# Gated cross-attention and a ternary feed-forward on one core: another order of the feed-forward tiles' steps, wider copies, and three products moved

## The chip, the cores and the metric

The kernel runs on one core of one Trainium2 chip. The metric is the device time of one execution in microseconds (us). The core has TensorE (PE; its weight loads are listed as PEld), VectorE (DVE), ScalarE (ACT), GpSimd (POOL) and SyncE (SP, which only issues DMAs here). Each engine takes its own instructions strictly in order; engines wait for one another on semaphores.

## The reference, cut to what matters

```python
# x [32, 224, 512], ctx [32, 750, 384], 16 heads; weights Wq, Wkv, w1 [2048, 512], w2 [512, 2048]
x = x + tanh(g_xattn) * attention(layernorm(x), ctx, mask)      # attention stage
x = x + tanh(g_ffn) * ffn(layernorm(x))                         # feed-forward stage

def bitlinear(x, w, b):
    x = x * rsqrt(mean(x * x) + 1e-5)                           # per row
    s = 127 / clip(max(abs(x)), 1e-5)                           # per row
    xq = clip(round(x * s), -128, 127) / s
    m = clip(mean(abs(w)), 1e-5)
    wq = clip(round(w / m), -1, 1) * m                          # three levels
    return xq @ wq.T + b
ffn = lambda x: bitlinear(gelu(bitlinear(x, w1, b1)), w2, b2)
```

There are 32 x 224 = 7168 rows, so 56 tiles of 128 rows in the feed-forward stage.

## The kernel before, in words

The **attention stage** (the first 1480 us or so) goes batch by batch and writes its rows, not yet gated, to a DRAM tensor `attn_d`. `divided` (L624) ends a batch: VectorE takes reciprocals of the denominators (`rden`, [57, 16]) and multiplies the rows out of PSUM. The last batch's rows, the row of the mean of v that SP spreads over a batch, and then a barrier stand before the next stage.

The **feed-forward stage** (L1116 on) is a software pipeline over the 56 tiles. `run_steps` (L1163) calls each engine's `step(s, j, u)`: some steps written out, a hardware loop of four steps per turn, some steps written out. In step s the work of several tiles is in flight. With k for a tile:

- SP loads x (`xb`) and attention rows (`ab`) of a tile into one of four slots and stores results from two slots of `yo`.
- GpSimd, tile s+2: gates `ab` (L1227), adds it to `xb` to give `x1` (L1229), computes the factor FAC by a power (L1234, L1237), centres the row, `xc` (L1242). Between, it adds the result of tile s-2 (`result`, L1215). For tile s: HR, a power of the mean square (L1246), and `x1b` = x1 + gated b2 (L1250).
- VectorE, tile s: four hidden copies `hid` = PSUM x XDEQ + b1, 512 columns each (L1302); the copy of the turned `xq` of s+1 (L1306) and half that of `hq` of s-1 (L1309); bn_stats and bn_aggr of s+2 (L1313, L1315), -mean (L1317); the maximum of |hid| over 2048 columns (L1321), HMS = mean square + eps (L1324), the maximum of |xc| (L1329); then for both tiles, interleaved, the small [128, 1] chains: CLIP, INV, DEQ, S (L1334 to L1355); and `xq` of s+2, rounded (L1360).
- ScalarE, tile s: four GELUs of 512 columns in place (L1264); the other half of the copy of turned `hq` of s-1 (L1267); the square of `hid` with its sum (L1272); `yo` of s-1 out of PSUM x HDEQ (L1278); `hq` = hid x HS, rounded (L1281).
- TensorE: 16 first matmuls of tile s in four groups of 512 columns (L1379); four transposes of `xq` of s+1 (L1387); 16 transposes of `hq` of s-1 (L1396), and right behind them its second matmul, 16 times 512 columns (L1406).

HDEQ is the clipped maximum / 127 x w_mean x gate; XDEQ the clipped maximum / 127 x w_mean. PSUM's eight banks: four hold the hidden tile, two the turned hq, one y, one the turned xq.

## Time and profile before

| what | us |
|---|---|
| median of 3 runs (lowest, highest) | 2026.45 (2025.77, 2028.01) |
| the profiled execution | 2027.01 |
| its span, first to last instruction | 2025.2 |
| busy in the span: PE / DVE / ACT / POOL | 1890.2 / 1285.2 / 1059.2 / 550.2 |
| granted TensorE clock, mean | 0.987 |

Views used below: the windows (busy time of each engine in a stretch), the timeline (one line per run of instructions of one line of code, with the idle time before it and what ended that in brackets), and the groups by form (one line of code and one shape: count, busy time, mean duration). An instruction can start before the one ahead of it on its engine has ended; so starts tell how long an engine is occupied, durations when a result is there.

### The profile page before, as it was taken

How to read it: one execution, taken by the hardware profiler on the slowest of the kernel's cores; microseconds unless marked ns; L12 is line 12 of the kernel's file. 1: busy time of each engine (PE TensorE's matmuls, PEld its weight loads, DVE VectorE, ACT ScalarE, POOL GpSimd, SP SyncE). 2: the span in 40 equal slices, each digit the busy share in tenths (PEclk: the TensorE clock that was granted, in tenths of full speed). 3: DMA queues.
4: the chain of work that ended last, by engine and by line, in shares of the span. 5: the costliest groups of instructions: out<-in, count | busy, mean ns of one | idle time of the engine just before them, and what ended most of it. 6: DMA issues, size and time to landing. Idle time of an engine off the chain costs nothing. (4 is left out here: it accounts for less than half of the span.)

```text
span 2025.2 us, 39793 instructions
## 1 busy us (share of the span) xinstructions
PE 1890.2 (93%) x13922; PEld 1469.5 (73%) x13923; DVE 1285.2 (63%) x2586; ACT 1059.2 (52%) x1807; POOL 550.2 (27%) x589
## 2 busy tenths in 40 slices
PE   4999999999999999999999999999849898898987
PEld 4888888888888887888888888888724444444444
DVE  3555455455545545555556545555559999999996
ACT  3444444444444443444444444444338888888887
POOL 2101011010101111010102101010037777777774
PEclk9999999999999999999999999999969999999999
DMA  3012111111211111112211111111022222222221
GB/s 123 19 50 80 49 47 42 47 42 49 76 53 47 42 47 43 48 45 60 73 42 47 42 47 42 47 57 47 21 88 79 93 78 93 78 93 83 88 87 49
DMA packets 56104, 120.61 MB, mean 60 GB/s; under 512 B 5597, under 2 KB 5597, under 8 KB 55934
## 3 DMA queue, kind: packets, MB, share of 16 engines
q1 hardware_dynamic: 56062, 120.07, 18.5%
q8 instruction: 24, 0.39, 0.1%
q14 instruction: 18, 0.15, 0.0%
HBM read 101.64 MB, written 29.43 MB: 65 GB/s over the span
## 5 line engine op out<-in xcount | busy, mean ns | idle before, releaser
L412 ACT ACTIVATE prob<-psum,nmax 114x750 f32<-114x750 f32 x256 | 225.4, 885 | 253.1 <-DVE nmax L600 253.1
L605 DVE TENSOR_TENSOR k_l<-psum,k_h 128x376 fp32r<-128x376 f32 (+1 forms) x256 | 140.2, 548 | 284.8 <-ACT k_h L403 284.2
L338 POOL TENSOR_TENSOR y_l<-y,y_h 128x750 fp32r<-128x750 f32 x96 | 161.8, 1708 | 551.5 <-ACT y_h L398 550.9
L403 ACT ACTIVATE k_h<-psum 128x376 fp32r<-128x376 f32 (+1 forms) x256 | 124.0, 485 | 354.3 <-PE psum L836 352.7
L600 DVE TENSOR_REDUCE nmax<-psum 114x1 f32<-114x750 f32 x256 | 228.4, 934 | 104.9 <-PE psum L825 102.5
L836 PE MATMUL psum<-y_h,wkv_h 128*128 128x376 f32 (+1 forms) x768 | 277.0, 361 | 1.1 <-DVE q_l L593 1.1
L836 PE MATMUL psum<-y_h,wkv_l 128*128 128x376 f32 (+1 forms) x768 | 255.9, 333 | 0.0
L836 PE MATMUL psum<-y_l,wkv_h 128*128 128x376 f32 (+1 forms) x768 | 255.7, 333 | 0.0
L1406 PE MATMUL psum<-w_q,hq_t 128*128 128x512 bf16 x896 | 205.0, 382 | 49.4 <-DVE hq_t L1309 49.3
L846 PE MATMUL psum<-wkv_h,y_h 128*125 128x512 f32 x576 | 237.0, 411 | 0.0
L846 PE MATMUL psum<-wkv_l,y_h 128*125 128x512 f32 x576 | 227.7, 395 | 0.0
L846 PE MATMUL psum<-wkv_h,y_l 128*125 128x512 f32 x576 | 227.0, 394 | 0.0
L614 DVE COPY prob_t<-psum 125x342 f32<-125x342 f32 x256 | 126.0, 509 | 153.8 <-PE psum L856 146.0
L1379 PE MATMUL psum<-w_q,xq_t 128*128 128x512 bf16 x896 | 204.6, 382 | 2.3 <-DVE xq_t L1306 2.3
L1406 PEld LDWEIGHTS psum<-w_q,hq_t 128*128 128x128 bf16 x896 | 84.2, 98 | 152.4 <-issue 60.7
L856 PEld LDWEIGHTS psum<-ident,prob 114*125 114x125 f32 x1536 | 186.4, 189 | 9.8 <-issue 2.7
L856 PE MATMUL psum<-ident,prob 114*125 114x114 f32 x1536 | 189.1, 273 | 2.8 <-ACT prob L412 2.8
L344 POOL TENSOR_SCALAR x_var<-x_mv 114x1 f32<-114x1 f32 x16 | 6.7, 421 | 646.1 <-DVE x_mv L578 646.1
L865 PE MATMUL psum<-prob_t,v 125*64 125x114 f32 x3072 | 181.5, 267 | 0.6 <-DVE prob_t L614 0.6
L865 PEld LDWEIGHTS psum<-prob_t,v 125*64 125x64 f32 x3072 | 153.4, 138 | 33.8 <-issue 33.0
L1379 PEld LDWEIGHTS psum<-w_q,xq_t 128*128 128x128 bf16 x896 | 88.0, 98 | 109.6 <-DVE xq_t L1306 2.8
L836 PEld LDWEIGHTS psum<-y_h,wkv_h 128*128 128x128 f32 x768 | 144.5, 188 | 23.1 <-DVE q_l L593 1.5
(117 smaller groups left out, 3351.9 us busy)
## 6 DMA issues: line engine op xcount, KB each, us to landing
y<-in_ctx_t SPq DMA_DIRECT2D x32, 1125.0 KB, 8.0
w_part<-in_w_t SPq DMA_DIRECT2D x32, 512.0 KB, 8.2
xb<-in_x SPq DMA_DIRECT2D x56, 256.0 KB, 2.7
ab<-attn_rows SPq DMA_DIRECT2D x56, 256.0 KB, 2.9
out_rows<-yo SPq DMA_DIRECT2D x56, 256.0 KB, 2.0
attn_rows<-vmean_rows SPq DMA_DIRECT2D x32, 336.0 KB
xa<-in_x SPq DMA_DIRECT2D x32, 112.0 KB
attn_rows<-attn SPq DMA_DIRECT2D x32, 112.0 KB
```

The costliest lines, as they stand in the source:

```text
L338: pool.tensor_tensor(y_l[:, slot, c, :], y[:, c, :], y_h[:, slot, c, :].bitcast(F32), ALU.subtract).then_inc(a_yl, 1)
L403: act.activation(k_h[:, g, s0:s1], ps_proj[k_bank[par][g, hf]][:, 0:s1 - s0], ACT.Copy).then_inc(a_kh, 1)
L412: act.activation(prob[:, e, :], ps_score[e][0:RP], ACT.Exp, bias=nmax[:, i:i + 1], accum_out=den[:, i:i + 1]).then_inc(p.exp, 1)
L600: dve.tensor_reduce(nmax[:, i:i + 1], ps_score[e][0:RP], AX.X, ALU.max, negate=True).then_inc(p.max, 1)
L605: dve.tensor_tensor(k_l[:, g, s0:s1], ps_proj[k_bank[par][g, hf]][:, 0:s1 - s0], k_h[:, g, s0:s1].bitcast(F32), ALU.subtract).then_inc(a_k ...
L614: dve.tensor_copy(prob_t[:, g % 2, e, MH:MJ, :].rearrange("p j n -> p (j n)"), ps_pt[e][1]).then_inc(p.pd, 1)
L836: mm = pe.matmul(out_, ws[:, c, w], ys[:, slot, c, s0:s1], start=(c == 0 and n == 0), stop=(c == CC - 1 and n == 2))
L846: mm = pe.matmul(out_, ys[:, slot, c, mcols], ws[:, c, D:], start=(c == 0 and n == 0), stop=(c == CC - 1 and n == 2))
L856: mm = pe.transpose(ps_pt[e][hf][:, RP * j:RP * j + RP], prob[:, e, MC * jj:MC * jj + MC], ident[0:RP, 0:RP])
L865: mm = pe.matmul(ps_o[PW * e:PW * e + PW, g, :], v[:, slot, j, w:w + PW], prob_t[:, g % 2, e, j, :], start=(j == 0), stop=(j == MJ - 1))
L1379: mm = pe.matmul(psum[:, i, :], xq_t[:, j % 2, 128 * c:128 * c + 128], w1_q[:, c, BANK * i:BANK * i + BANK], start=(c == 0), stop=(c == DC ...
L1406: mm = pe.matmul(ps_y, hq_t[:, p, 128 * c:128 * c + 128], w2_q[:, c, :], start=(c == 0), stop=(c == FC - 1))
```

## The change

What it does, beside the diff:

- The gate of attention moves from the feed-forward stage (GpSimd, `ab` x gate, [128, 512] for each tile) into `divided`: `rden` x gate, [57, 16] for each batch, with a wait for the gates once.
- Order of a step: TensorE does the first matmul of tile s, the transposes of hq of s-1, those of xq of s+1, then the second matmul of s-2. ScalarE: `yo` of s-3, `hq` of s-1, two GELUs of 1024 columns, copy of turned hq, square. VectorE: the H chain of tile s-1 first, then bn_stats and bn_aggr of s+2, two hidden copies of 1024 columns, the copies of turned hq and xq, maximum of |xc| and the X chain, and last the maximum of |hid| of tile s. GpSimd: HMS (new there) and HR of s-1, `x1b` of s, the result of s-3, `xc` and FAC of s+2, `x1` of s+3, and `xq` of s+2 (new there).
- The hidden copy's factor is XCLIP, the clipped maximum itself. b1 is scaled once by 127 / w_mean, and GELU's scale, a [128, 1] column, brings w_mean / 127 back. XDEQ and -mean go. b1's scaling is one VectorE instruction over 2048 columns in step 0.
- `x1b` and `cols` have four slots; each result is stored a step later, and each load is issued a turn further ahead of the stores in SP's queue.

```diff
                     dve.wait_ge(p.rows, n + 1 + ONE)
                     dve.reciprocal(rden[:], ps_den).then_inc(own_dve, 1)
                     dve.wait_ge(own_dve, 1)
+                    dve.tensor_scalar(rden[:], rden[:], gates[0:RM, 0:1], 1.0, ALU.mult, ALU.mult).then_inc(own_dve, 1)
+                    dve.wait_ge(own_dve, 2)
                     dve.wait_ge(p.st, stored)
                     dve.tensor_tensor(attn[:].rearrange("p (m e d) -> p m e d", m=NP, e=2),
                                       ps_rows.rearrange("p (m e d) -> p m e d", m=NP, e=2),
...
                 moments(last, 0, 32 + ONE)
                 normalise(last, 0, RB)
+                dve.wait_ge(a_gate, 1)
 
...
         def run_steps(eng, step):
-            full = (NT - 2) // NX
-            for s in range(-2, NX):
-                step(s, s, 0)
-            with eng.Fori(1, full) as u:
+            for s in range(-3, NX):
+                step(s, s % NX, 0)
+            with eng.Fori(1, NT // NX - 1) as u:
                 for j in range(NX):
                     step(eng.snap(u * NX + j), j, u)
-            for s in range(full * NX, NT + 2):
-                step(s, s - full * NX, full)
+            for s in range(NT - NX, NT + 4):
+                step(s, s % NX, s // NX)
...
-                with sp.Fori(1, NT // NX) as u:
+                for k in range(NX, 2 * NX):
+                    sp.wait_ge(t_x1, k - NX + 1)
+                    load(k, k % NX)
+                with sp.Fori(2, NT // NX) as u:
                     for j in range(NX):
                         sp.wait_ge(t_x1, u * NX + j - NX + 1)
                         load(u * NX + j, j)
-                        store(u * NX + j - NX, j % 2)
-                for k in range(NT - NX, NT):
+                        store(u * NX + j - 2 * NX, j % 2)
+                for k in range(NT - 2 * NX, NT):
                     store(k, k % 2)
...
+                def sums(s, j, u):
+                    k = s + 3
+                    slot = (j + 3) % NX
+                    pool.wait_ge(b_ld[slot], 32 * (u + (j + 3) // NX + 1) if not isinstance(s, int) else 32 * (k // NX + 1))
+                    pool.sem_inc(met_pool, 1)
+                    if exists(k - NX):
+                        pool.wait_ge(t_x1b, k - NX + 1)
+                        pool.wait_ge(t_xc, k - NX + 1)
+                        pool.sem_inc(met_pool, 1)
+                    pool.tensor_tensor(x1[:, slot, :], xb[:, slot, :], ab[:, slot, :], ALU.add).then_inc(t_x1, 1)
...
+                    k = s - 1
+                    if exists(k):
+                        c = cols[:, (j - 1) % NX, :]
+                        pool.wait_ge(t_ss, k + 1)
+                        pool.sem_inc(met_pool, 1)
+                        pool.tensor_scalar(c[:, HMS:HMS + 1], c[:, HSS:HSS + 1], 1.0 / F, RMS_EPS, ALU.mult, ALU.add).then_inc(own_ms, 1)
+                        pool.wait_ge(own_ms, 1)
+                        pool.tensor_tensor(c[:, HR:HR + 1], c[:, HMS:HMS + 1], half[:], ALU.pow).then_inc(t_hr, 1)
+                        pool.sem_clear(own_ms)
+                    if exists(s):
+                        if exists(s - NX):
+                            pool.wait_ge(t_yo, s - NX + 1)
+                            pool.sem_inc(met_pool, 1)
+                        pool.wait_ge(t_x1, s + 1)
+                        pool.sem_inc(met_pool, 1)
+                        pool.tensor_tensor(x1b[:, j % NX, :], x1[:, j % NX, :], b2_gated[:], ALU.add).then_inc(t_x1b, 1)
+                    k = s - 3
+                    if exists(k):
+                        half_, slot = (j - 3) % 2, (j - 3) % NX
+                        pool.wait_ge(t_ye, k + 1)
+                        pool.wait_ge(t_x1b, k + 1)
+                        pool.sem_inc(met_pool, 1)
+                        pool.tensor_tensor(yo[:, half_, :], yo[:, half_, :], x1b[:, slot, :], ALU.add).then_inc(t_yo, 1)
                     k = s + 2
...
+                        slot, c, h = (j + 2) % NX, cols[:, (j + 2) % NX, :], j % 2
+                        pool.wait_ge(t_mv, k + 1)
+                        if exists(k - 2):
+                            pool.wait_ge(t_xq, k - 1)
                         pool.sem_inc(met_pool, 1)
...
+                        pool.tensor_scalar(xc[:, h, :], x1[:, slot, :], x_mv2[:, h, 0:1], 1.0, ALU.subtract, ALU.mult).then_inc(t_xc, 1)
...
+                    if exists(s + 3):
+                        sums(s, j, u)
+                    if exists(k):
+                        pool.wait_ge(t_xs, k + 1)
+                        if exists(k - 2):
+                            pool.wait_ge(t_xt, k - 1)
+                        pool.sem_inc(met_pool, 1)
+                        pool.tensor_scalar(xq[:, h, :], xc[:, h, :], c[:, XS:XS + 1], ROUND_HALF, ALU.mult, ALU.add).then_inc(t_xq, 1)
...
+                    k = s - 3
+                    if exists(k):
+                        half_, c = (j - 3) % 2, cols[:, (j - 3) % NX, :]
+                        act.wait_ge(t_y, k + 1)
+                        if exists(k - 2):
+                            act.wait_ge(b_st[half_], 16 * (k // 2) if isinstance(s, int) else 16 * (2 * u + (j - 3) // 2))
+                        act.activation(yo[:, half_, :], ps_y, ACT.Copy, scale=c[:, HDEQ:HDEQ + 1]).then_inc(t_ye, 1)
+                    k = s - 1
+                    if exists(k):
+                        h, c = (j - 1) % 2, cols[:, (j - 1) % NX, :]
+                        act.wait_ge(t_hs, k + 1)
+                        if exists(k - 2):
+                            act.wait_ge(t_ht, 2 * (k - 2) + 2)
+                        act.activation(hq[:, h, :], hid[:, h, :], ACT.Identity, scale=c[:, HS:HS + 1],
+                                       bias=round_col[:]).then_inc(t_hq, 1)
...
+                        for i in range(2):
+                            seg = hid[:, j % 2, FU * i:FU * i + FU]
+                            act.wait_ge(t_he, 2 * s + i + 1)
+                            act.activation(seg, seg, ACT.Gelu, scale=gelu_in[:, 0:1]).then_inc(t_g, 1)
+                    k = s - 1
+                    if exists(k):
+                        act.wait_ge(t_ht, 2 * k + 2)
+                        if exists(k - 2):
+                            act.wait_ge(t_y, k - 1)
                         act.activation(hq_t[:, (j - 1) % 2, F // 2:], ps_ht[1], ACT.Copy, bias=-HALF_BIAS).then_inc(t_ha, 1)
...
+                        act.wait_ge(t_g, 2 * s + 2)
...
+                        act.activation(junk[:], hid[:, j % 2, :], ACT.Square,
+                                       accum_out=cols[:, j % NX, HSS:HSS + 1]).then_inc(t_ss, 1)
...
+                    if isinstance(s, int) and s == 0:
                         dve.wait_ge(b_bias, 32)
-                    if hidden:
+                        dve.tensor_scalar(b1_row[:], b1_row[:], bias_out[:], LEVELS, ALU.mult, ALU.mult).then_inc(b_b1, 1)
+                        dve.wait_ge(b_b1, 1)
+                    k = s - 1
+                    if exists(k):
+                        c = cols[:, (j - 1) % NX, :]
+                        dve.wait_ge(t_hr, k + 1)
+                        dve.wait_ge(t_max, k + 1)
+                        dve.tensor_scalar(c[:, HCLIP:HCLIP + 1], c[:, HMAX:HMAX + 1], c[:, HR:HR + 1], CLIP,
+                                          ALU.mult, ALU.max).then_inc(own_h, 1)
+                        dve.wait_ge(own_h, 1)
+                        dve.reciprocal(c[:, HINV:HINV + 1], c[:, HCLIP:HCLIP + 1]).then_inc(own_h, 1)
+                        dve.tensor_scalar(c[:, HDEQ:HDEQ + 1], c[:, HCLIP:HCLIP + 1], 1.0 / LEVELS, w_gated[:],
+                                          ALU.mult, ALU.mult).then_inc(own_h, 1)
+                        dve.wait_ge(own_h, 3)
+                        dve.tensor_scalar(c[:, HS:HS + 1], c[:, HINV:HINV + 1], LEVELS, c[:, HR:HR + 1],
+                                          ALU.mult, ALU.mult).then_inc(t_hs, 1)
+                        dve.sem_clear(own_h)
+                    if exists(s + 2):
+                        moments(s, j)
+                    if exists(s):
...
+                        for i in range(2):
+                            n = slice(FU * i, FU * i + FU)
+                            dve.wait_ge(t_h, 2 * s + i + 1)
+                            dve.scalar_tensor_tensor(out=hid[:, j % 2, n], in0=ps_h[i], scalar=c[:, XCLIP:XCLIP + 1],
                                                      in1=b1_row[:, n], op0=ALU.mult, op1=ALU.add).then_inc(t_he, 1)
+                    k = s - 1
+                    if exists(k):
+                        dve.wait_ge(t_ht, 2 * k + 1)
+                        if exists(k - 2):
+                            dve.wait_ge(t_y, k - 1)
+                        dve.tensor_scalar(hq_t[:, (j - 1) % 2, 0:F // 2], ps_ht[0], HALF_BIAS, 1.0,
+                                          ALU.subtract, ALU.mult).then_inc(t_hd, 1)
...
+                        dve.wait_ge(t_xc, k + 1)
                         dve.tensor_reduce(c[:, XMAX:XMAX + 1], xc[:, j % 2, :], AX.X, ALU.max,
-                                          apply_absolute_value=True).then_inc(own_cols, 1)
-                    if hidden:
...
+                                          apply_absolute_value=True).then_inc(own_x, 1)
+                        dve.wait_ge(t_fac, k + 1)
+                        dve.wait_ge(own_x, 1)
                         dve.tensor_scalar(c[:, XCLIP:XCLIP + 1], c[:, XMAX:XMAX + 1], c[:, FAC:FAC + 1], CLIP,
...
+                                          ALU.mult, ALU.max).then_inc(own_x, 1)
+                        dve.wait_ge(own_x, 2)
+                        dve.reciprocal(c[:, XINV:XINV + 1], c[:, XCLIP:XCLIP + 1]).then_inc(own_x, 1)
+                        dve.wait_ge(own_x, 3)
...
+                                          ALU.mult, ALU.mult).then_inc(t_xs, 1)
+                        dve.sem_clear(own_x)
+                    if exists(s):
+                        dve.wait_ge(t_g, 2 * s + 2)
+                        dve.tensor_reduce(cols[:, j % NX, HMAX:HMAX + 1], hid[:, j % 2, :], AX.X, ALU.max,
+                                          apply_absolute_value=True).then_inc(t_max, 1)
...
+                                pe.wait_ge(t_he, 2 * (s - 1) + i + 1)
+                            for o in range(2):
+                                at_ = FU * i + BANK * o
+                                for c in range(DC):
+                                    mm = pe.matmul(ps_h[i][:, BANK * o:BANK * o + BANK], xq_t[:, j % 2, 128 * c:128 * c + 128],
+                                                   w1_q[:, c, at_:at_ + BANK], start=(c == 0), stop=(c == DC - 1))
                             mm.then_inc(t_h, 1)
+                    k = s - 1
+                    if exists(k):
+                        pe.wait_ge(t_hq, k + 1)
+                        for g in range(2):
+                            if exists(k - 1):
+                                pe.wait_ge((t_hd, t_ha)[g], k)
+                            for c in range(FC // 2):
+                                mm = pe.transpose(ps_ht[g][:, 128 * c:128 * c + 128],
+                                                  low_halves(hq[:, (j - 1) % 2, :], FC // 2 * g + c), ident_h[:])
+                            mm.then_inc(t_ht, 1)
...
+                    k = s - 2
+                    if exists(k):
+                        if exists(k - 1):
+                            pe.wait_ge(t_ye, k)
                         for c in range(FC):
                             if c == 0:
-                                pe.wait_ge(t_hd, s)
+                                pe.wait_ge(t_hd, k + 1)
                             if c == FC // 2:
-                                pe.wait_ge(t_ha, s)
-                            mm = pe.matmul(ps_y, hq_t[:, p, 128 * c:128 * c + 128], w2_q[:, c, :],
+                                pe.wait_ge(t_ha, k + 1)
+                            mm = pe.matmul(ps_y, hq_t[:, j % 2, 128 * c:128 * c + 128], w2_q[:, c, :],
                                            start=(c == 0), stop=(c == FC - 1))
                         mm.then_inc(t_y, 1)
```

## Rows read from the trace of the kernel before

**Rows 1.** Windows: window, length, busy PE, PEld, DVE, ACT, POOL; PEclk, DMA share, GB/s.

```profile
50.00:1400.00 1350.00, 1332.38 (x10343) 1149.55 (x10341) 724.59 (x1294) 583.04 (x1219) 169.61 (x120) 1.00 0.16 49
...
1502.85:2004.07 501.22, 447.53 (x2823) 232.26 (x2822) 487.14 (x1146) 421.12 (x494) 354.90 (x432) 0.99 0.24 81
```

**Rows 2.** Timeline, one steady tile: start us, us, engine, line, op, [idle <-releaser].

```profile
1704.44 2.71 DVE L1302 SCALAR_TENSOR_TENSOR hid<-psum,cols,b_row 128x512 f32<-128x512 f32 x4
...
1705.84 2.18 ACT L1264 ACTIVATE hid<-hid 128x512 f32<-128x512 f32 x4
...
1707.92 1.00 ACT L1267 ACTIVATE hq_t<-psum 128x1024 bf16<-128x1024 f16 x1
1708.01 0.68 DVE L1313 BATCH_NORM_STATS2 x_st<-x 128x6 f32<-128x512 f32 x1
...
1708.23 3.61 PE L1406 MATMUL psum<-w_q,hq_t 128*128 128x512 bf16 x16 [0.84 <-DVE hq_t L1309]
...
1708.72 0.18 DVE L1315 BATCH_NORM_AGGREGATE x_mv<-x_st 128x2 f32<-128x6 f32 x1
1708.83 1.90 ACT L1272 ACTIVATE junk<-hid 128x2048 bf16<-128x2048 f32 x1
...
1708.94 0.15 DVE L1317 TENSOR_SCALAR cols<-x_mv 128x1 f32<-128x1 f32 x1
...
1709.29 0.19 POOL L1234 TENSOR_SCALAR cols<-x_mv 128x1 f32<-128x1 f32 x1 [1.61 <-DVE cols L1317]
1709.57 0.55 POOL L1237 TENSOR_TENSOR cols<-cols,half 128x1 f32<-128x1 f32 x1
...
1710.63 0.19 ACT L1272 ACTIVATION_READ_ACCUMULATOR junk<-hid 128x1 f32 x1
...
1712.86 2.10 ACT L1281 ACTIVATE hq<-hid,round_col,cols 128x2048 f32<-128x2048 f32 x1 [0.29 <-DVE cols L1350]
...
1713.47 2.71 DVE L1302 SCALAR_TENSOR_TENSOR hid<-psum,cols,b_row 128x512 f32<-128x512 f32 x4
```

**Rows 3.** Timeline: VectorE's hidden copies right after the loop's back edge.

```profile
1577.03 2.73 DVE L1302 SCALAR_TENSOR_TENSOR hid<-psum,cols,b_row 128x512 f32<-128x512 f32 x4 [0.26 <-PE psum L1379]
```

**Rows 4.** Groups by form, VectorE: xcount | busy us, mean ns | idle before, releaser.

```profile
L1321 DVE TENSOR_REDUCE cols<-hid 128x1 f32<-128x2048 f32 x56 | 128.0, 2286 | 0.4 <-ACT hid L1264 0.3
...
L1329 DVE TENSOR_REDUCE cols<-xc 128x1 f32<-128x512 f32 x56 | 37.8, 676 | 3.5 <-POOL xc L1242 3.5
```

**Rows 5.** Groups by form, ScalarE.

```profile
L1264 ACT ACTIVATE hid<-hid 128x512 f32<-128x512 f32 x224 | 123.5, 617 | 0.3
...
L407 ACT ACTIVATE v<-psum 125x512 f32<-125x512 f32 x96 | 57.5, 599 | 123.3 <-PE psum L846 123.3
...
L1278 ACT ACTIVATE yo<-psum,cols 128x512 f32<-128x512 f32 x56 | 38.5, 687 | 69.1 <-PE psum L1406 69.1
```

**Rows 6.** Groups by form, GpSimd.

```profile
L1227 POOL TENSOR_SCALAR ab<-ab,gates 128x512 f32<-128x512 f32 x56 | 48.0, 857 | 3.8 <-DMA ab<-attn_rows 3.6 <-POOL b_gated L1208 0.2
L1242 POOL TENSOR_SCALAR xc<-x,cols 128x512 f32<-128x512 f32 x56 | 38.9, 695 | 0.0
```

**Rows 7.** Timeline, second last tile: HR on GpSimd, then VectorE's chain behind it.

```profile
2002.34 0.55 POOL L1246 TENSOR_TENSOR cols<-cols,half 128x1 f32<-128x1 f32 x1 [5.42 <-DVE cols L1324]
...
2002.92 0.21 DVE L1334 TENSOR_SCALAR cols<-cols 128x1 f32<-128x1 f32 x1 [0.66 <-POOL cols L1246]
...
2003.17 0.17 DVE L1343 RECIPROCAL cols<-cols 128x1 f32<-128x1 f32 x1
2003.25 0.20 DVE L1348 TENSOR_SCALAR cols<-cols,w_gated 128x1 f32<-128x1 f32 x1
```

**Rows 8.** Timeline, drain: last tile's hidden copies and its last sum.

```profile
2004.07 3.27 DVE L1302 SCALAR_TENSOR_TENSOR hid<-psum,cols,b_row 128x512 f32<-128x512 f32 x4 [0.49 <-PE psum L1379]
...
2021.50 1.26 POOL L1215 TENSOR_TENSOR yo<-yo,x1b 128x512 f32<-128x512 f32 x1 [7.41 <-ACT yo L1278]
```

**Rows 9.** Timeline, head: GpSimd's first product, with VectorE idle.

```profile
1489.82 0.70 POOL L1227 TENSOR_SCALAR ab<-ab,gates 128x512 f32<-128x512 f32 x1 [3.56 <-DMA ab<-attn_rows]
```

More of the change, by code:

```diff
@@ L54, in gated_cross_attention_bit_ffn @@
     assert 2 * DC == QTR and DC * F == FC * D and QTR % 2 == 0 and HPG == 4 and NG == 4 and CC == 3
[L55 removed]
+    assert RP <= 128 and MC * MJ == M and NT * 128 == ROWS and NT % NX == 0 and FU == 2 * BANK
     assert (F * D) & (F * D - 1) == 0
@@ L1136, in gated_cross_attention_bit_ffn @@
         yo = sb("yo", [128, 2, D])
-        (NEGM, FVAR, FAC, XMAX, XCLIP, XINV, XS, XDEQ, HSS, HMS, HR, HMAX, HCLIP, HINV, HS, HDEQ) = range(16)
+        (FVAR, FAC, XMAX, XCLIP, XINV, XS, HSS, HMS, HR, HMAX, HCLIP, HINV, HS, HDEQ) = range(14)
         halves = psum[:].bitcast(F16)
+        ps_h = [banks[:, FU * i:FU * i + FU] for i in range(2)]
         ps_ht = [halves[:, 4 + g, :] for g in range(2)]
@@ L1287, in _, with moments @@
             def _(dve):
+                dve.reciprocal(bias_out[:], w_mean[:, 0:1]).then_inc(b_wg, 1)
                 dve.tensor_tensor(w_gated[:], w_mean[:, 1:2], gates[:, 1:2], ALU.mult).then_inc(b_wg, 1)
-                dve.wait_ge(b_wg, 1)
+                dve.tensor_scalar(gelu_in[:], w_mean[:, 0:1], 1.0 / LEVELS, 1.0, ALU.mult, ALU.mult).then_inc(b_wg, 1)
+                dve.wait_ge(b_wg, 3)
+                def moments(s, j):
+                    k, slot, h = s + 2, (j + 2) % NX, j % 2
+                    dve.wait_ge(t_x1, k + 1)
+                    dve.bn_stats(x_st[:, h, :], x1[:, slot, :]).then_inc(own_st, 1)
+                    dve.wait_ge(own_st, 1)
+                    dve.bn_aggr(x_mv2[:, h, :], x_st[:, h, :]).then_inc(t_mv, 1)
+                    dve.sem_clear(own_st)
@@ L1336, in step @@
-                    if ahead:
-                        dve.wait_ge(t_fac, s + 3)
-                        dve.wait_ge(own_cols, h + x)
-                        dve.tensor_scalar(c[:, XCLIP:XCLIP + 1], c[:, XMAX:XMAX + 1], c[:, FAC:FAC + 1], CLIP,
-                                          ALU.mult, ALU.max).then_inc(own_cols, 1)
-                    if hidden:
-                        dve.wait_ge(own_cols, h + x + h)
-                        dve.reciprocal(c[:, HINV:HINV + 1], c[:, HCLIP:HCLIP + 1]).then_inc(own_cols, 1)
@@ L1344, in step @@
-                    if ahead:
-                        dve.wait_ge(own_cols, 2 * (h + x))
-                        dve.reciprocal(c[:, XINV:XINV + 1], c[:, XCLIP:XCLIP + 1]).then_inc(own_cols, 1)
-                    if hidden:
-                        dve.tensor_scalar(c[:, HDEQ:HDEQ + 1], c[:, HCLIP:HCLIP + 1], 1.0 / LEVELS, w_gated[:], ALU.mult, ALU.mult)
-                        dve.wait_ge(own_cols, 2 * (h + x) + h)
-                        dve.tensor_scalar(c[:, HS:HS + 1], c[:, HINV:HINV + 1], LEVELS, c[:, HR:HR + 1], ALU.mult, ALU.mult).then_inc(t_hs, 1)
```

149 lines of the change are left out of this document (20 added, 129 removed).

## The prediction

> **What bounds the kernel now.** I read the busy time by stretch first. In the attention stage TensorE is busy 1332 of 1350 us; the feed-forward stage, from the first hidden copy of tile 0 to that of tile 55, takes 501.2 us, in which VectorE is busy 487 us, TensorE 448, ScalarE 421, GpSimd 355 [rows 1]. So each of the 55 intervals takes 501.2 / 55 = 9.11 us, and VectorE fills it. The timeline of one tile says the same: its first hidden copy starts at 1704.44, the next tile's at 1713.47, 9.03 us later, and nearly every VectorE instruction between them starts when the one before ends; TensorE idles 0.84 us before its second matmul, ScalarE before hq [rows 2]. Every fourth interval is longer, at the loop's back edge, where the copy stands idle 0.26 us after a short instruction [rows 3]; 4 x (9.11 - 9.03) = 0.33 us each time.
>
> **The change on each engine, for a tile.** VectorE loses -mean, HMS, XDEQ and xq: by starts in the timeline about 0.11 + 0.06 + 0.12 + 0.41 = 0.7 us (xq lasts 0.49, overlapped by 0.08). Its copies of 1024 save two fixed parts: four of 512 take 2.71 us; one has 0.737, of which 512 columns are 512 x (2286 - 676) / 1536 ns = 0.537 by the two reductions of 2048 and 512 [rows 4], so one of 1024 has 1.27, occupies 1.19 (0.08 overlap with the next), and two end after 2.46. That is 0.25 less. It pays for small chains no longer interleaved: HCLIP, HINV, HDEQ, HS alone take 0.76, XCLIP, XINV, XS some 0.6. I sum 8.4 us of VectorE work. TensorE keeps its instructions: 3.45 + 3.45 for 32 matmuls of 512 and 1.1 for 20 transposes, 8.1 us with small gaps; its second matmul of tile s-2 no longer waits for a copy of the same step, so the 0.84 us before it go, but TensorE isn't the bound. ScalarE's GELU gets two instructions for four, and a scale from a column. Without it 1024 columns would take 0.617 + 512 x (1899 - 617) / 1536 ns = 1.044 us; the scale's price I take from a plain PSUM copy of 512 (599 ns) against the same with a column scale (687): 0.09 [rows 2, 5]. So 1.13 each, occupying 1.04 (0.10 overlap, from four GELUs in 2.18): two are 2.08, what four take now, and the wider GELU brings nothing. GpSimd loses ab x gate (0.86), gains HMS (0.19) and xq; xq is bounded by xc (0.695, one column, same shape) and by ab (0.857), and I take 0.70, being nearest in form [rows 6]. Its sum is 6.7 to 7.1, with room.
>
> **The ring that takes over.** VectorE's 8.4 would be the step if nothing waited. But GELU(s), square(s), HMS, HR, HCLIP(s) and then, behind it in VectorE's queue, the hidden copy of s+1 form a ring over three engines. HR's end to HCLIP took 0.03 to 0.04 in the tail, HCLIP to HINV start 0.25, HDEQ 0.08 later [rows 7]; HS waits for HDEQ's end, so HS starts at 0.56 and, 0.12 on, bn_stats at 0.68. bn_stats to bn_aggr is 0.71 (rows: 1708.01, 1708.72), aggr 0.12, copy one starts at 1.51, copy two at 2.70 and ends at 3.97. GELU two starts 0.04 later and occupies 1.04; hq_t's copy occupies 0.91 (1707.92 to 1708.83), the square with its accumulator read 1.99 (to 1710.82) [rows 2]. GpSimd begins HMS 0.21 after a signal it passes through its meeting count (1709.09 to 1709.29), HMS to HR is 0.28 (L1234 to L1237), HR lasts 0.55, HCLIP comes 0.04 later. Sum: 3.97 + 0.04 + 1.04 + 0.91 + 1.99 + 0.21 + 0.28 + 0.55 + 0.04 = **9.03 us**. The ScalarE branch of the ring (HS ends 0.76, hq 2.01, both GELUs 2.08, then as before) gives 8.87 and hides behind it. So VectorE idles some 0.6 us ahead of HCLIP, ScalarE over 1 us ahead of hq, GpSimd 1.1 ahead of HMS, and these idle times swallow the back edge. The step goes from 9.11 to 9.03: the 0.7 us taken from VectorE turn into waiting for HR. Were the ring's cover for the back edge missing, 0.33 / 4 = 0.08 would return.
>
> TensorE stays ahead: hq ends at 2.9 in this step, 16 transposes and 4 to 4.1, second matmul to 7.5, the next first matmul's first half to 9.4, needed at 10.5. GpSimd in queue order: x1b, the sum of tile s-3 (moved, with its store on SP one step later; loads of tile s+8 are issued ahead of stores, four steps before use), xc, the factor, x1 of s+3, xq; its wait for XS ends at 6.4, done by 7.1, HMS comes at 8.2.
>
> **Outside the steady steps.** Attention: one small product of [57, 16] in `divided`, 0.20 + 0.04 us, 32 times. TensorE's next scores don't need what is queued behind it (k_l of the last half waits for ScalarE anyway): zero to 0.05 us each, I take zero for 31. The last one stands on the path to the stage's last store: +0.25. The wait for the gates costs nothing: ScalarE writes them ahead of the work that VectorE's normalising must wait for. Head: ab x gate (0.70 and 0.08 up to the sum) no longer stands before the first x1 [rows 9], nor before tile 1's; against this, xq(0) queues on GpSimd behind x1(1), and b1 is scaled once on VectorE (2048 columns, four times xq's 0.49 at most, or 3 us beside a GpSimd sum), mostly under the first matmuls. Laying the first tiles out with the durations above gives -1.6; bounds -2.5 and 0. The last step has no moments between chain and copies, -0.8 (0.71 + 0.12). Drain: now 18.7 us from the last tile's first copy (2004.07) to its sum's end (2022.76) [rows 2, 8]. After, second matmul of tile 54 stands between transposes and second matmul of 55: +3.5; hq of 55 some 0.6 later: +4.1, bounds 3.3 and 5.
>
> A rule bears on b1's scaling: by the Trainium skill, "SBUF — State Buffer", "SBUF: two separate sides", VectorE in a two-port mode and GpSimd lock each other out for a whole instruction. The traces agree as far as ab goes: 0.857 us in the steady steps, where it starts while VectorE's xq runs, and 0.70 in the head, where VectorE is idle [rows 6, 9]. By it b1's scaling could stand behind one GpSimd sum, +1.3 once; the sum of terms without it is unchanged.
>
> **Sum.** Steps 55 x (9.03 - 9.11) = -4.6; head -1.6; the last step -0.8; drain +4.1; attention's end +0.25: -2.65 us. The profiled execution took 2027.0 us (span 2025.2 and 1.8 around it), 0.6 above the median, 2026.45. So 2023.8; I say **2024**.
>
> **Rivals.**
> 1. The ring is shorter: copy two or the column scale costs less, and ScalarE's branch sets 8.87, or less. 55 x -0.16 more is -9: 2015. For it: overlaps could be larger; against: all its durations are read. 0.20.
> 2. No ring: HR comes in time and VectorE's 8.4 or TensorE's 8.1 is the step, 55 x -0.6 more: 1985 to 1991. It needs 0.6 us off a chain of durations measured one by one. 0.04.
> 3. Slower: the back edge shows on the ring. It is met on three engines, each 0.33 every fourth step, and only VectorE's is bound today. If ScalarE's and GpSimd's aren't swallowed, 0.25 per tile: 55 x 0.25 = +14 on 2024, 2038; one more of them +5, 2029. It decides from +0.12 us a step. Against it: each ends in a wait of 0.6 us or more. 0.16.
> 4. The forecast, ring near 9.03 with 0.06 either way and head and drain within bounds: 2019 to 2029. 0.60.
>
> **How the numbers follow.** 0.2% is 4 us, about what can be told from no change. The forecast's case is faster beyond that for a quarter of its weight (0.14), slower hardly (0.03). Faster 0.20 + 0.04 + 0.14 = 0.38; slower 0.15 + 0.03 = 0.18; same 0.44. The range takes in rival 1's 2015 and the milder half of rival 3: 2014 to 2031.
>
> **What would show it.** After: intervals of about 9.03 us, with none longer at the back edge; VectorE idle 0.6 us ahead of HCLIP, released by GpSimd's HR; copies of 1024 at 1.27, GELU at 1.13, xq on GpSimd at 0.70; no idle TensorE ahead of the second matmul, some ahead of hq's transposes; the drain 22 to 24 us. Wrong if HCLIP doesn't wait for HR, if a copy or GELU differs by over 0.1 us, or if intervals of 9.3 return.

## The result, and the profile after

The kernel after takes **2036.98 us** (median; 2035.77 to 2042.23), beside 2026.41 us for the kernel before on the same chip: a ratio of 1.0058, 95% interval [1.0042, 1.0073]. It is slower by 10.6 us where 2.4 less was forecast. The first thing to read is the page's head and its busy times (PE, PEld, DVE, ACT, POOL), of the kernel after:

```profile
span 2035.3 us, 39425 instructions
...
PE 1887.2 (93%) x13865; PEld 1464.8 (72%) x13923; DVE 1258.3 (62%) x2285; ACT 1063.3 (52%) x1695; POOL 624.1 (31%) x644
```

The span grew by 10.1 us (2025.2 before). Next the windows of the kernel after, in the columns of [rows 1]: the attention stage, and the stretch from the first hidden copy of tile 0 to that of tile 55.

```profile
50.00:1400.00 1350.00, 1332.42 (x10341) 1149.51 (x10340) 728.69 (x1324) 582.93 (x1219) 169.59 (x120) 1.00 0.16 49
1502.97:2008.39 505.42, 440.90 (x2754) 226.02 (x2807) 454.88 (x817) 424.45 (x382) 424.74 (x488) 0.99 0.23 79
```

VectorE's busy time fell from 487 to 455 us, and yet the stretch grew from 501.22 to 505.42: VectorE is no longer what fills it. GpSimd's grew from 355 to 425, more than xq and HMS account for. TensorE's granted clock in the stretch is 0.99 in both kernels, and the attention stage is unchanged (TensorE busy 1332.4 of 1350 us, clock 1.00). One steady tile of the kernel after, in the timeline (start us, us, engine, line, operation, idle before):

```profile
1704.35 0.21 DVE L1336 TENSOR_SCALAR cols<-cols 128x1 f32<-128x1 f32 x1 [0.56 <-POOL cols L1230]
...
1704.91 0.21 DVE L1343 TENSOR_SCALAR cols<-cols 128x1 f32<-128x1 f32 x1
1705.09 0.69 DVE L1321 BATCH_NORM_STATS2 x_st<-x 128x6 f32<-128x512 f32 x1
1705.15 2.10 ACT L1289 ACTIVATE hq<-hid,round_col,cols 128x2048 f32<-128x2048 f32 x1 [1.28 <-DVE cols L1343]
...
1705.82 0.18 DVE L1323 BATCH_NORM_AGGREGATE x_mv<-x_st 128x2 f32<-128x6 f32 x1
1706.03 2.48 DVE L1355 SCALAR_TENSOR_TENSOR hid<-psum,cols,b_row 128x1024 f32<-128x1024 f32 x2
...
1707.34 2.34 ACT L1295 ACTIVATE hid<-hid,gelu_in 128x1024 f32<-128x1024 f32 x2
...
1708.43 3.62 PE L1433 MATMUL psum<-w_q,hq_t 128*128 128x512 bf16 x15
...
1709.59 1.00 ACT L1301 ACTIVATE hq_t<-psum 128x1024 bf16<-128x1024 f16 x1
...
1710.49 1.90 ACT L1306 ACTIVATE junk<-hid 128x2048 bf16<-128x2048 f32 x1
...
1712.68 0.19 POOL L1228 TENSOR_SCALAR cols<-cols 128x1 f32<-128x1 f32 x1 [0.96 <-ACT junk L1306]
1712.95 0.55 POOL L1230 TENSOR_TENSOR cols<-cols,half 128x1 f32<-128x1 f32 x1
...
1713.54 0.21 DVE L1336 TENSOR_SCALAR cols<-cols 128x1 f32<-128x1 f32 x1 [0.55 <-POOL cols L1230]
```

HCLIP (L1336) starts at 1704.35 and again at 1713.54: a step of 9.19 us, with VectorE idle 0.55 us ahead of HCLIP, and HR (L1230) the releaser. L1343 is HS. Against the tile of [rows 2] the idle TensorE ahead of its second matmul is gone. The steady intervals (from one tile's first hidden copy to the next one's) are 9.19 us, and 9.26 at the loop's back edge. The waits of 1560 to 1980 us (engine, line, what it waited for: total us, times, longest) show who stands idle over 45 or 46 tiles:

```profile
ACT hq L1289 <- DVE cols L1343: 59.7, 45, 1.4
...
POOL cols L1228 <- ACT junk L1306: 44.2, 46, 1.0
DVE cols L1336 <- POOL cols L1230: 25.0, 45, 0.6
```

VectorE, ScalarE and GpSimd wait for one another in turn: a ring, and no engine that is full.

**Where the 10.1 us stand.** GpSimd's first feed-forward instruction starts at 1489.05 (before 1489.82, [rows 9]): -0.77. From there to the first hidden copy 13.92 us against 13.03: +0.89. The 55 intervals: +4.20. The drain, from tile 55's first copy to its sum's end, 2008.39 to 2032.82, 24.43 against 18.69: +5.74.

The head, in GpSimd's timeline of the kernel after:

```profile
1489.05 1.26 POOL L1216 TENSOR_TENSOR x<-xb,ab 128x512 f32<-128x512 f32 x1 [3.38 <-DMA ab<-attn_rows]
1491.55 2.00 POOL L1253 TENSOR_SCALAR xc<-x,x_mv 128x512 f32<-128x512 f32 x1 [1.23 <-DVE x_mv L1323]
...
1496.86 2.00 POOL L1253 TENSOR_SCALAR xc<-x,x_mv 128x512 f32<-128x512 f32 x1 [0.47 <-DVE x_mv L1323]
...
1500.98 1.67 POOL L1266 TENSOR_SCALAR xq<-xc,cols 128x512 f32<-128x512 f32 x1
```

xc takes 2.00 us. Before it took 0.695 [rows 6]; the diff turned it from a sum with the negated mean into a difference with the mean, so that the negation could go, and my prediction passed over that line. VectorE was idle from 1491.33 to 1493.59, so it is no contention with VectorE.

The drain, in the timeline of the kernel after (TensorE and the last sum):

```profile
2019.44 1.89 PE L1414 MATMUL psum<-ident_h,hq 128*128 128x128 f16 x16 [4.31 <-ACT hq L1289]
...
2021.12 5.11 PE L1433 MATMUL psum<-w_q,hq_t 128*128 128x512 bf16 x16
...
2027.01 3.63 PE L1433 MATMUL psum<-w_q,hq_t 128*128 128x512 bf16 x15 [0.78 <-ACT yo L1282]
...
2031.56 1.26 POOL L1245 TENSOR_TENSOR yo<-yo,x1b 128x512 f32<-128x512 f32 x1 [3.14 <-ACT yo L1282]
```

Tile 54's second matmul stands between tile 55's transposes and its second matmul. It costs more than the 3.5 us put down for it: TensorE idled 4.31 us ahead of the transposes, and its granted clock is 0.50 from 2019 to 2023 us (1.2 GHz, the lower of its two levels), so these 16 matmuls take 5.11 us, not 3.62; then tile 55's wait 0.78 us for ScalarE to empty the one PSUM bank of y. The kernel before met the lower level at the same place: there the clock is 0.60 and 0.55 in the two stretches of 2 us from 2014, the transposes take 1.89 us too, and the last tile's second matmul right behind them 4.28. In the kernel after tile 54's takes that part, and tile 55's runs in 3.63.

### The profile page after: what moved, and what is told of

It reads as the page before. It is cut to its first block and busy times, and to the rows that moved or that the text cites. A ratio compares the mean times of both kernels' runs of the same rounds, so it can differ in the third digit from the quotient of the medians.

```text
span 2035.3 us, 39425 instructions
## 1 busy us (share of the span) xinstructions
PE 1887.2 (93%) x13865; PEld 1464.8 (72%) x13923; DVE 1258.3 (62%) x2285; ACT 1063.3 (52%) x1695; POOL 624.1 (31%) x644
## 5 line engine op out<-in xcount | busy, mean ns | idle before, releaser
L1433 PE MATMUL psum<-w_q,hq_t 128*128 128x512 bf16 x841 | 200.8, 381 | 3.7 <-ACT yo L1282 0.8
L1289 ACT ACTIVATE hq<-hid,round_col,cols 128x2048 f32<-128x2048 f32 x56 | 117.3, 2095 | 75.5 <-DVE cols L1343 75.5
```

Of the source, the lines that this page charges most:

```text
L1433: mm = pe.matmul(ps_y, hq_t[:, j % 2, 128 * c:128 * c + 128], w2_q[:, c, :], start=(c == 0), stop=(c == FC - 1))
```

## The experiments

The theory by now: the step is the ring of the prediction (HCLIP, moments, two copies, second GELU, hq_t copy, square, HMS, HR), 9.19 instead of 9.03; head and drain as above. The rivals: GpSimd's slow xc is on the path, VectorE's own work is, or the ring's extra 0.16 us has another cause. Each ratio is to the kernel before on the same chip. The intervals of some ratios overlap that of the kernel after (1.0042 to 1.0073): those of xc as a sum, of four copies, and of the clears. There the steps in the trace decide, not the time.

**GpSimd's xc as a sum again** (of the kernel after):

```diff
- pool.tensor_scalar(xc, x1, x_mv2[:, h, 0:1], 1.0, ALU.subtract, ALU.mult)
+ pool.tensor_scalar(NEGM, x_mv2[:, h, 0:1], -1.0, 1.0, ALU.mult, ALU.mult)
+ pool.tensor_scalar(xc, x1, NEGM, 1.0, ALU.add, ALU.mult)
```

> The changed kernel, but GpSimd negates the mean ([128, 1]) and centres the row by adding it, as before, where the change subtracts the mean (2.00 us an instruction against 0.695). The ring theory (square, HMS, HR on GpSimd, HCLIP to HS, bn_stats, bn_aggr and two hidden copies on VectorE, second GELU, hq_t copy on ScalarE, 9.19 us a step) has the centring off the ring: xc back at about 0.70, GpSimd's wait before HMS longer by 1.0 us, the step stays at 9.19 to 9.21 and only the head gains 1 to 2 us: 2035 to 2036. The rival, that GpSimd's slow subtraction makes the step, has the step fall to 9.0 to 9.1: 2026 to 2031.

Measured: 2035.73 us, ratio 1.0054 [1.0038, 1.0071]. xc in the head, in GpSimd's timeline, and one of GpSimd's waits in the steady steps (1560 to 1980 us):

```profile
1493.25 0.69 POOL L1256 TENSOR_SCALAR xc<-x,cols 128x512 f32<-128x512 f32 x1
```

```profile
POOL xq L1270 <- DVE cols L1384: 54.1, 46, 1.2
```

xc is back at 0.69 us, for one [128, 1] instruction of 0.19. The head from GpSimd's first instruction (1490.48) to the first copy (1502.27) is 11.79 us, 2.13 less than after's 13.92. The steps stay at 9.18 and 9.25: what GpSimd saves it spends waiting for XS, 54.1 us where it had waited 2.0. So the slow instruction costs the head 2.1 us, and the steps nothing.

**HMS taken out of the ring.** HR becomes the power of the bare sum of squares (F and its root move into the constants of HCLIP and HDEQ), which leaves out the 1e-5 under the root:

```diff
- pool.tensor_scalar(HMS, HSS, 1.0 / F, RMS_EPS, ALU.mult, ALU.add)
- pool.tensor_tensor(HR, HMS, half, ALU.pow)
+ pool.tensor_tensor(HR, HSS, half, ALU.pow)
```

> The changed kernel without HMS: HR is the power of the bare sum of squares, the factor sqrt(2048) goes into HCLIP and HDEQ, and the 1e-5 under the root is left out. The ring theory: 0.27 us less on the ring, so the step falls from 9.19 to about 8.93 and the time by 54 x 0.27 = 14 to 2022 or 2023, with VectorE's wait before HCLIP falling from 0.55 to 0.3. The rival, VectorE (8.6 us of work and its own waits) or GpSimd as the bound: no more than 0.05 a step, 2034 to 2037.

Measured: 2020.58 us, ratio 0.9973 [0.9964, 0.9983]. Steps of 8.90 and 8.98: 0.29 us less, for an instruction that occupies 0.27 (1712.68 to 1712.95 above); the time is just below the 2022 expected. VectorE's wait shrinks by the same amount a tile (25.0 / 45 = 0.56 to 12.6 / 47 = 0.27):

```profile
DVE cols L1333 <- POOL cols L1228: 12.6, 47, 0.3
```

A 0.19 us instruction on an engine that is busy 31% of the span moves the kernel by 16 us (55 x 0.29). The ring sets the step.

**xq back on VectorE:**

```diff
- pool.tensor_scalar(xq, xc, XS, ROUND_HALF, ALU.mult, ALU.add)      # end of GpSimd's step
+ dve.wait_ge(own_x, 4)
+ dve.tensor_scalar(xq, xc, XS, ROUND_HALF, ALU.mult, ALU.add)       # behind XS, ahead of max |hid|
```

> The changed kernel with xq back on VectorE, right behind XS and ahead of the maximum of |hid|. The ring theory: its 0.45 us fit into the 0.55 us that VectorE waits for HR, so the step stays within 9.19 to 9.28 and the time within 2035 to 2041. The rival that VectorE's work sets the step: 55 x 0.45 = 25 us more, 2062.

Measured: 2045.32 us, ratio 1.0099 [1.0082, 1.0116]; steps of 9.34 and 9.41. VectorE's timeline, from XS to HCLIP:

```profile
1704.77 0.21 DVE L1374 TENSOR_SCALAR cols<-cols 128x1 f32<-128x1 f32 x1
1705.09 0.48 DVE L1379 TENSOR_SCALAR xq<-xc,cols 128x512 f32<-128x512 f32 x1
1705.49 2.28 DVE L1383 TENSOR_REDUCE cols<-hid 128x1 f32<-128x2048 f32 x1
1707.88 0.21 DVE L1330 TENSOR_SCALAR cols<-cols 128x1 f32<-128x1 f32 x1
```

This lies outside both ranges that I had given, 2035 to 2041 for the ring and 2062 for a VectorE that sets the step. HCLIP no longer waits for HR: VectorE is full. XS to the maximum is 0.72 us, and was 0.13 (1710.58 to 1710.71 in the kernel after): xq costs 0.59, as it also waits for XS and delays what follows. So VectorE's own work without xq is 9.34 - 0.6 = 8.74 us a step, not the 8.4 of my sum. I had read the 0.55 us that VectorE stands idle ahead of HCLIP as room; 0.11 of it stands there even when VectorE is full (1707.77 to 1707.88), and xq needs more than the rest. Moving xq to GpSimd is worth 8 us to the kernel after; the move is right, and the ring hides the rest of its worth.

**Four copies and four GELUs of 512 columns**, as before:

```diff
- for i in range(2): n = slice(1024 * i, 1024 * i + 1024)
+ for i in range(4): n = slice(512 * i, 512 * i + 512)      # TensorE's waits, copies, GELUs
```

> The changed kernel with four hidden copies and four GELUs of 512 columns again (and TensorE's groups of 512). The ring theory: the copies end 0.23 later, but the GELU behind the last one is 0.45 shorter, so the branch over VectorE falls to 8.98, while the branch over hq and the GELUs on ScalarE grows by 0.32 from 8.87 to 9.19: the step stays near 9.2, 2034 to 2038. The rival, that the widening saves what the engines' sums say: 0.23 to 0.32 a step more, 2049 to 2055.

Measured: 2040.97 us, ratio 1.0072 [1.0056, 1.0089], above the 2034 to 2038 expected. ScalarE's hq and GELUs, and VectorE's copies:

```profile
1707.40 2.10 ACT L1290 ACTIVATE hq<-hid,round_col,cols 128x2048 f32<-128x2048 f32 x1 [1.28 <-DVE cols L1344]
...
1708.27 2.72 DVE L1356 SCALAR_TENSOR_TENSOR hid<-psum,cols,b_row 128x512 f32<-128x512 f32 x4
...
1709.40 2.54 ACT L1296 ACTIVATE hid<-hid,gelu_in 128x512 f32<-128x512 f32 x4
```

The copies cost 0.24 us more, the GELUs 0.20. But the GELUs do not wait for the copies now: the first starts at 1709.40, right behind hq, with the first copy long done, and ScalarE is idle nowhere from hq to the square. So ScalarE's branch of the ring (HS, hq, four GELUs) is the longer one, as the theory had it. From HCLIP (1706.59) to the hq_t copy (1711.85) it is 5.26 us, and 5.24 in the kernel after. The steps are 9.20 to 9.30, mean 9.25, and the 55 intervals 508.0 us against 505.4. They alternate because hq starts 0.25 us behind HS's start in two steps of four and 0.34 in the other two; it does so in the kernel after as well, where VectorE's branch is longer and hides it. What makes the 0.34 stays open. So the wider shapes bring 2.6 us over 55 tiles. The head is 13.92 us, as in the kernel after: the first copy comes 1.4 us later (1504.37) because the stage started 1.4 us later (1490.45 against 1489.05), which is not the shapes' doing. The drain is 25.24 us, 0.8 longer.

**ScalarE's hq_t copy moved behind the square:**

```diff
+ act.activation(junk, hid, ACT.Square, accum_out=HSS)      # tile s
  act.activation(hq_t, ps_ht[1], ACT.Copy)                  # tile s-1
- act.activation(junk, hid, ACT.Square, accum_out=HSS)
```

> The changed kernel with one ScalarE instruction moved: the copy of turned hq (0.90 us) goes from between the second GELU and the square to behind the square. Nothing needs it before the next step's second matmul. The ring theory: both branches of the ring lose 0.90 (9.19 to 8.29 over VectorE), and VectorE's own work becomes the step, 8.6 to 8.75 us with the back edge showing again: 2037 - 54 x 0.45 to 0.55, so 2007 to 2013. The rival, that the later copy delays TensorE (second matmul, or the transposes that need its bank) and turns into a new wait: 2025 or more.

Measured: **2014.70 us**, ratio 0.9952 [0.9936, 0.9969], just above the 2007 to 2013 expected. Steps of 8.74 and 8.82. The copy (0.90 on the ring) is needed by the second matmul only. VectorE's timeline, the maximum of |hid| and HCLIP:

```profile
1711.41 2.28 DVE L1385 TENSOR_REDUCE cols<-hid 128x1 f32<-128x2048 f32 x1
1713.80 0.21 DVE L1336 TENSOR_SCALAR cols<-cols 128x1 f32<-128x1 f32 x1
```

No idle time ahead of HCLIP: of the 0.90 us the ring lost, the step gains 0.45, and then VectorE's 8.74 takes over, the value that the run of xq on VectorE had given by subtraction.

**VectorE's clears once in four steps.** In the kernel after, VectorE clears a semaphore behind HS and behind bn_aggr, each in front of work of the ring. Here they are done once in four steps, and the waits count up:

```diff
- dve.wait_ge(own_st, 1); dve.bn_aggr(...); dve.sem_clear(own_st)
+ dve.wait_ge(own_st, j + 1); dve.bn_aggr(...)
+ if j == NX - 1: dve.sem_clear(own_st)                     # own_h alike
```

> The changed kernel, but VectorE clears its two own semaphores (of the H chain and of bn_stats to bn_aggr) once in four steps instead of in every step, with higher counts to wait for. Theory: the 0.15 us a step by which the ring is longer than forecast stands where VectorE's queue handles a clear and further waits between short instructions (HS to bn_stats 0.18 instead of 0.12, bn_aggr to the first copy 0.21 instead of 0.12); without the clears three steps of four lose about 0.1: 2032 to 2035. Rival: these starts are 0.18 and 0.21 apart for the instructions' own sake, and nothing changes: 2037.

Measured: 2032.98 us, ratio 1.0038 [1.0025, 1.0052]. Steps of 9.02, 9.03, 9.18, 9.23. A step without clears, in VectorE's timeline (HCLIP, HS, bn_stats, bn_aggr, copies):

```profile
1704.07 0.21 DVE L1337 TENSOR_SCALAR cols<-cols 128x1 f32<-128x1 f32 x1 [0.55 <-POOL cols L1230]
...
1704.62 0.21 DVE L1345 TENSOR_SCALAR cols<-cols 128x1 f32<-128x1 f32 x1
1704.76 0.68 DVE L1321 BATCH_NORM_STATS2 x_st<-x 128x6 f32<-128x512 f32 x1
1705.47 0.18 DVE L1323 BATCH_NORM_AGGREGATE x_mv<-x_st 128x2 f32<-128x6 f32 x1
1705.58 2.47 DVE L1358 SCALAR_TENSOR_TENSOR hid<-psum,cols,b_row 128x1024 f32<-128x1024 f32 x2
```

From HCLIP to the first copy 1.51 us, the number of my sum, and the step is 9.02, my 9.03. With the clears it is 1.68 and 9.19: the mis-sized term is found. The difference is 0.04 to 0.05 us behind HS, 0.10 behind bn_aggr, and 0.02 between bn_stats and bn_aggr. The fourth step, whose copy follows the back edge, gains only 0.03 (9.23 for 9.26): bn_aggr to the copy takes 0.31 there, and why is open. The 55 intervals are 501.9 us against 505.4, as two of the first ones are longer, 9.70 and 9.95. A kernel with no clear at all was not run.

The clear is not the whole cause. In the hardware loop a wait's value is computed in VectorE's queue from the loop's counter; in the steps written out it is a constant. These instructions of the queue show in the views by source line (kernel after, durations in ns; 48 is once in each step of the loop; L1320 is the wait ahead of bn_stats, L1345 the clear behind HS, L1354 the wait ahead of the copies):

```profile
L1320 DVEq ALU_OP  x48: 40/40/40, 1539.2 to 1972.1; - x48
L1345 DVEq EVENT_SEMAPHORE_RANGE_CLEAR  x56: 54/54/54, 1511.5 to 2017.1; - x56
L1354 DVEq FUSED_REGOPS  x48: 46/46/46, 1540.2 to 1973.0; - x48
```

A step written out near the end, with both clears and without the computed values (HS, bn_stats, bn_aggr, copies):

```profile
1981.16 0.21 DVE L1343 TENSOR_SCALAR cols<-cols 128x1 f32<-128x1 f32 x1
1981.29 0.69 DVE L1321 BATCH_NORM_STATS2 x_st<-x 128x6 f32<-128x512 f32 x1
1982.01 0.18 DVE L1323 BATCH_NORM_AGGREGATE x_mv<-x_st 128x2 f32<-128x6 f32 x1
1982.19 2.48 DVE L1355 SCALAR_TENSOR_TENSOR hid<-psum,cols,b_row 128x1024 f32<-128x1024 f32 x2
```

| steps | HS to bn_stats, us | bn_aggr to copy, us |
|---|---|---|
| in the loop, clear and computed value | 0.18 | 0.21 |
| in the loop, computed value alone | 0.13 | 0.11 |
| written out, clear, and a constant to wait for | 0.13 | 0.18 |

So one such instruction between two short ones costs nothing behind HS, and the clear and the computed value together cost 0.05. That is also why the two intervals written out with moments at the end are 9.10 and 9.11, not 9.19.

**The second matmul ahead of the transposes behind the last tile:**

```diff
+ if s >= NT: second(s)          # second matmul of s-2
  transposes of hq, s-1
- second(s)
+ if s < NT: second(s)
```

> The kernel after, with one edit: in the steps behind the last tile TensorE issues the second matmul ahead of the transposes. It measures the drain's term by itself. If the second matmul of tile 54 standing between transposes and second matmul of tile 55 is what lengthened the drain, the drain from tile 55's first copy to its sum's end goes from 24.4 us to 20.5 to 21.7 (in late_sum_tail, where copies and square are exchanged too, it was 19.7, and 22.7 in copy_late without this edit, so 3.0 less), steps stay at 9.19 with 9.26 at the back edge, and the time is 2033 to 2034.5. Rival: the drain is held by ScalarE's and VectorE's chain (square, HR, hq, transposes, copy, and the transfer out), and TensorE's order is covered: drain over 24 us and 2036.5 to 2037.5.

Measured: 2031.45 us, ratio 1.0027 [1.0018, 1.0036]. TensorE's timeline in the drain:

```profile
2015.51 3.63 PE L1405 MATMUL psum<-w_q,hq_t 128*128 128x512 bf16 x16 [0.93 <-ACT yo L1282]
2018.97 1.06 PE L1430 MATMUL psum<-ident_h,hq 128*128 128x128 f16 x16
```

The drain is 19.70 us, 4.73 less than after's and 1.0 more than before's. The gain is more than I expected (a drain of 20.5 to 21.7, and 2033 to 2034.5 us), since tile 54's matmul now fills the pause ahead of the transposes, the granted clock stays at 1.00 there, and the transposes take 1.06 instead of 1.89 us. The steps are as in the kernel after.

**The gate moved, alone, in the kernel before.** The product with the gate leaves GpSimd, and `divided` gets its small one:

```diff
+ dve.tensor_scalar(rden, rden, gates[0:RM, 0:1], 1.0, ALU.mult, ALU.mult)
- pool.tensor_scalar(ab, ab, gates[:, 0:1], 1.0, ALU.mult, ALU.mult)
```

> The kernel before with the gate alone moved: rden x gate in the attention stage, no product of ab and gate on GpSimd. GpSimd is not on the path of the steps there, so they stay at 9.03 and 9.36; the head loses 0.8 us, the end of attention takes 0.25 more: 2025 to 2027, which can't be told from before. If the small product delayed TensorE in each of 32 batches it would be 2030 or more.

Measured: 2024.25 us, ratio 0.9997 [0.9986, 1.0007]: no difference that can be told. The steps stay at 9.03 and 9.35, and the head is 12.38 us for 13.03, 0.65 of the 0.8 expected. The 32 small products and the 56 larger ones lie beside other work, but for those of the head.

**Together.** Copy late, xc as a sum, and the drain's order:

> The changed kernel with three edits: the copy of turned hq behind the square, the row centred by adding a negated mean on GpSimd, and, in the steps after the last tile, the second matmul ahead of the transposes. The ring theory with the measured head and drain: steps as in the run with the copy alone, 1 to 2 us less in the head (two first centrings of 2.00 us) and 3 to 4 less in the drain (tile 54's second matmul done before hq of 55 is there): 2003 to 2008. If the head's and the drain's terms are wrong it equals the run with the copy alone.

Measured: 2007.26 us, ratio 0.9919 [0.9899, 0.9938]; steps 8.74 and 8.82, drain 19.73. And with the clears once in four steps on top:

> The kernel of late_sum_tail with VectorE's two clears (own_st, own_h) done once in four steps as in clear_fourth. In late_sum_tail no wait stands ahead of VectorE in the steady steps (0.4 us in 48 steps), so its own work is the step: 8.74 us, 8.82 at the back edge. If VectorE is the bound there and each clear occupies its queue, three steps of four lose what they lost in clear_fourth (9.19 to 9.02, so 0.16): steps of 8.58, 8.58, 8.72, 8.80, mean 8.67 against 8.76, so 55 x 0.09 = 5 us less: 2001 to 2003. Rival: the clears cost only as a delay on the ring that waits for HR, and in a step that has no such wait they are covered: steps stay at 8.74, time 2006 to 2008, as late_sum_tail's 2007.3.

Measured: **2001.14 us**, ratio 0.9882 [0.9865, 0.9900]; steps of 8.58, 8.58, 8.75, 8.78 (mean 8.67). The rival falls: VectorE is full there, and the clears are part of its work. This beats the kernel before by 1.2% and, by the two ratios to it, the kernel after by 1.8%.

## Why the prediction was wrong

- **The ring: right, and its size was wrong.** Bound, place and releaser of the wait came out as forecast, shown by taking HMS out (-0.29 us a step) and by moving the hq_t copy. What failed are two starts in the sum, "bn_stats at 0.68" (0.12 behind HS) and "aggr 0.12". The prediction names no row for either, and [rows 2] has none. In the trace of before, 0.12 us is the distance between two [128, 1] instructions of the chain, which no clear parts; bn_aggr's next start, -mean, comes 0.22 behind it (1708.72 to 1708.94), and the maximum 0.11 behind -mean, in spite of a clear (the maximum, then XS and XDEQ):

```profile
1709.05 2.29 DVE L1321 TENSOR_REDUCE cols<-hid 128x1 f32<-128x2048 f32 x1
...
1712.75 0.20 DVE L1353 TENSOR_SCALAR cols<-cols 128x1 f32<-128x1 f32 x1
1712.87 0.20 DVE L1355 TENSOR_SCALAR cols<-cols,w_mean 128x1 f32<-128x1 f32 x1
```

  In the new order a clear and a computed wait stand behind HS and again behind bn_aggr. Measured 0.18, 0.73, 0.21: HCLIP to first copy 1.68, not 1.51. All other terms fit within 0.03: copies 2.48 (3.97 - 1.51 = 2.46), the second GELU 0.03 behind the last copy's end, GELU 1.06, hq_t copy 0.90, square 2.00, HMS's start 0.19, HMS 0.27, HR to HCLIP 0.59. So 9.19 instead of 9.03: 55 x 0.16 = 8.8 us. The run with clears once in four steps shows the cause in the steps without a back edge, 9.02 again.
- **The back edge** was to vanish; 0.07 us of 0.33 are left every fourth step, about 1 us: behind bn_aggr one more computed value stands there (L1351, 12 times, once a turn), and the copy starts 0.28 behind it instead of 0.21. Rival 3 had the right sign, but its mechanism gave only this. The first two intervals, 9.48 and 9.47, add 0.5 on top.
- **The last step, -0.8**: the two steps without moments give intervals of 8.25 and 8.84, 1.3 less together than two of 9.19; the two before them 9.10 and 9.11. Together that is some 1.5, and the sum had 0.8; here it erred by 0.7 in the kernel's favour.
- **Head, -1.6 forecast, +0.89 measured.** The step that failed is an omission: xc's new form, 2.00 us for 0.695, twice on the path. With xc as a sum the head is 11.79 us, against 13.03 - 1.6 = 11.4 of the forecast. The rest I put down to b1's scaling, which was to lie under the first matmuls; no run shows it by itself. It takes 1.70 us on VectorE, and the moments of tile 2 and the first copy start right behind it, some 1.6 to 2 us after the first eight matmuls, the ones that this copy needs (one record is missing there, so the ninth starts at 1500.95 or at 1501.38):

```profile
1500.39 1.70 DVE L1329 TENSOR_SCALAR b_row<-b_row,bias_out 128x2048 f32<-128x2048 f32 x1
1502.13 0.69 DVE L1321 BATCH_NORM_STATS2 x_st<-x 128x6 f32<-128x512 f32 x1
...
1502.97 1.28 DVE L1355 SCALAR_TENSOR_TENSOR hid<-psum,cols,b_row 128x1024 f32<-128x1024 f32 x1
```

- **The lock** between VectorE and GpSimd showed, on the other side: at 1500.98 GpSimd's xq took 1.67 us instead of 0.69 beside this scaling, which itself took 1.70, under four times the 0.49 of xq. From the scaling's end (1502.09) to xq's (1502.65) it is 0.56 us, 0.13 less than xq takes alone. The trace agrees, to 0.13 us, with the Trainium skill, "SBUF — State Buffer", "SBUF: two separate sides": the engine that comes second waits for the other's whole instruction. The page says it of VectorE instructions in a two-port mode; no run shows whether the scaling is one. I had the engine that waits the wrong way round. This xq is not on the path to the first copy.
- **Drain, +4.1 forecast, +5.74 measured.** Tile 54's second matmul in the way was the right cause, and hq of 55 comes 0.61 later, as forecast. The term that failed is the 3.5 us: they are 5.11, as the lower clock level fell on them; 0.65 of that is saved on the last matmul, 3.63 for 4.28. The wait of 0.78 for y's bank was missed. Reordering took 4.73 off.
- **Attention's end**, +0.25: GpSimd started 0.77 us earlier instead, but the run of xc as a sum, with the same attention stage, started at 1490.48, later than before. Over all runs with this attention stage the start lies between 1486.86 and 1490.81: the term is below what one execution can show, and so is the -0.77 (which the sum below carries).
- **VectorE's own work, 8.4**: 8.74, by the run with the copy late and, through subtraction, by that with xq on VectorE. 0.16 of the 0.34 goes with the clears (8.58); the rest is not traced to an instruction. So rival 2 (no ring) had its price wrong: from 9.03 to 8.74 it is 55 x 0.29 = 16 us, 2008, and not 1985 to 1991.
- **Widths and xq on GpSimd** came out as forecast: GELU 1.15 (1.13), copy 1.28 (1.27), xq 0.70. The wider GELU was to bring nothing, and against four with the same column scale it saves 0.20 us of ScalarE's time.

In sum: 10.1 measured against -2.65; of the 12.7 us between, 9.6 are the intervals (8.8 of them the two starts), 2.5 the head, 1.6 the drain, and -1.0 the stage's start. The time moved the other way than forecast because of the first three.

## What to carry to other kernels

When work is taken from a full engine, sum the longest ring through all engines, and take each start-to-start distance from a pair of rows with the same semaphore instructions and computed waits between them: two distances short by 0.06 and 0.09 us, taken from no row, were most of 8.8 us here, out of 12.7. On such a ring, first move what nobody on it needs (the hq_t copy, worth some 22 us) and only then shorten operations. And read each line of the diff for its operation, not only for its place: a difference is not a sum.
